# Attention and mixture of experts on one core: the products for the constant rows moved from one block in step 1 to eight groups in step 0, and the key rows cleared later

## What is computed

```python
attn = softmax(where(causal, -inf, q @ k.T * scale)); seq_out = attn @ v
x = layernorm(x + (seq_out + gated * mem_val) @ out_w.T + out_b)
h = gelu(x @ w1[e] + b1[e]); y = h @ w2[e] + b2[e]                # e = 0..3
c = einsum('eh,ehd->ed', gelu(b1), w2) + b2                      # one constant row for each expert
c_sum = c.sum(axis=0)
out = sum_k gates[k] * (y[topk[k]] - c[topk[k]] + c_sum)
x = layernorm(x + out)
```

## Time and profile before

| | |
|---|---|
| median of 3 runs | 1021.79 us (1018.55 to 1023.22) |
| the profiled execution | 1023.56 us, its span 1021.9 us |
| PE, PEld busy | 922.9 us (90%), 672.6 us (66%) |
| DVE, ACT, POOL busy | 736.5 us (72%), 595.0 us (58%), 425.8 us (42%) |
| mean granted TensorE clock | 0.961 of full |

### The profile page before, as it was taken

The page is one execution under the profiler, slowest core; times in us unless marked ns, Lnnn a source line. Parts: engine busy times, 40 slices in busy tenths (PEclk is TensorE's granted clock), DMA queues, the critical chain, the costliest instruction groups (busy, mean ns, idle before and its releaser), DMA issues. The chain is left out here.

```text
span 1021.9 us, 26568 instructions
## 1 busy us (share of the span) xinstructions
PE 922.9 (90%) x7976; PEld 672.6 (66%) x7977; DVE 736.5 (72%) x2689; ACT 595.0 (58%) x1357; POOL 425.8 (42%) x389
## 2 busy tenths in 40 slices
PE   4688999998899999999997989999999999999960
PEld 1244666656556666576564678888889978888850
DVE  4727789897787898989987677775655676555564
ACT  3246465564463555645555578676577756666663
POOL 6417144464183544644445534332222253233333
PEclk9789999999899999999999999999999999999985
DMA  4875203304114123041040543233223233233265
GB/s 147 259 203 141 64 23 95 96 22 141 51 53 137 43 89 102 1 137 53 22 146 2 184 163 82 51 48 49 43 43 71 47 85 53 42 52 52 39 191 180
DMA packets 60086, 89.48 MB, mean 88 GB/s; under 512 B 8636, under 2 KB 49488, under 8 KB 58928
## 3 DMA queue, kind: packets, MB, share of 16 engines
q1 hardware_dynamic: 44952, 61.80, 20.7%
q0 software_dynamic: 13728, 21.90, 11.3%
q10 hardware_dynamic: 1280, 4.19, 1.1%
HBM read 52.26 MB, written 35.47 MB: 86 GB/s over the span
## 5 line engine op out<-in xcount | busy, mean ns | idle before, releaser
L2007 DVE CUSTOM_DVE_ANT_0 junk<-sm,mask_ts 128x512 bf16<-128x512 f32 (+3 forms) x512 | 219.6, 486 | 59.4 <-PE sm L1405 58.0
L1145 ACT ACTIVATE arena_b<-st 128x512 f32<-128x512 f32 x320 | 180.2, 598 | 112.1 <-PE st L1367 111.0
L987 POOL DMA_INDIRECT sums<-arena_b x64 | 112.6, 1759 | 253.3 <-DVE arena_b L2241 243.3
L2203 DVE TENSOR_TENSOR arena_b<-arena_b 128x256 f16<-128x256 f32 (+1 forms) x280 | 116.1, 428 | 96.3 <-ACT arena_b L1221 93.9
L1365 PE MATMUL st<-arena_a 128*128 128x384 f16 (+3 forms) x512 | 127.0, 305 | 13.2 <-DMA arena_a<-max_row 7.5
L1405 PE MATMUL sm<-arena_a 128*128 128x512 f16 (+3 forms) x512 | 113.9, 310 | 12.8 <-DVE maxes L2007 6.5
L1556 PE MATMUL st<-arena_b,arena_a 128*128 128x256 f16 (+1 forms) x840 | 112.3, 271 | 6.4 <-DVE arena_b L1887 4.9
L1569 PE MATMUL pv<-arena_a,arena_b 128*128 x816 | 112.3, 274 | 0.0
L1556 PE MATMUL sm<-arena_b,arena_a 128*128 128x256 f16 (+1 forms) x840 | 110.7, 268 | 0.0
L1569 PE MATMUL sm<-arena_a,arena_b 128*128 x792 | 109.4, 274 | 0.0
L1217 ACT ACTIVATE arena_b<-sm,arena_b 128x256 f32<-128x256 f32 (+1 forms) x140 | 65.5, 468 | 65.8 <-PE sm L1556 50.6
(11 more groups left out here) (364 smaller groups left out, 1740.3 us busy)
## 6 DMA issues: line engine op xcount, KB each, us to landing
arena_b<-slots SPq DMA_DIRECT2D x32, 260.0 KB, 2.7
arena_a<-w SPq DMA_DIRECT2D x8, 1024.0 KB, 6.0
arena_b<-x_tr SPq DMA_DIRECT2D x8, 512.0 KB, 4.0
q_rows<-arena_b SPq DMA_DIRECT2D x32, 128.0 KB
k_rows<-arena_b SPq DMA_DIRECT2D x32, 128.0 KB
arena_a<-q_rows SPq DMA_DIRECT2D x32, 128.0 KB
arena_a<-k_rows SPq DMA_DIRECT2D x32, 128.0 KB
res<-x_tok POOLq DMA_DIRECT2D x8, 512.0 KB, 4.3
```

The costliest lines, as they stand in the source:

```text
L987: pool.indirect_dma_start(sums, bass.IndirectOffsetOnAxis(ap=token_now[:, 1 - par, m:m + 1], axis=0), y_out[1 - par][:, m, :], None, compu ...
L1145: act.activation(probs[:, q, :], st_ps[piece % 2][:, :], ACT.Exp, scale=SCORE_SCALE).then_inc(exp_done, 1)
L2007: last = dve.tensor_tensor_reduce(junk[:, n % 3, at:at + width], sm_ps[n % 3][:, at:at + width], mask_ts[:, T - width:T], 1.0, NEG, ALU.ad ...
L2203: dve.tensor_tensor(g_lo[par][:, hc, 0:rows], g_32[:, hc % 4, 0:rows], g_hi[par][:, hc, 0:rows], ALU.subtract).then_inc(hid_done, 1)
```

## The change

There are two parts.

First, the block of step 1 becomes eight groups in step 0. Stage `nothing` exists in step 0 and takes a number m from 0 to 7: group m is expert m // 2 and half m % 2 of its chunks, so four products, and it waits for its own transfer on `raw_in[m]` instead of `w2_in`, which is gone (the later use of `raw_in` in `weights` counts from 32). The groups stand in the list behind maxima 8, 10, 11, 13, 14 and 16, and the last two behind `maxima_rows`. ScalarE's copy stays where it was in step 1, as a stage of its own, `nothing_out`. Second, GpSimd waits for `dve_const` 4, VectorE's last instruction of the weights' split (L1646), before it clears `k_st[0]`; all that stands behind on GpSimd follows.

```diff
-        ("o_tokens", 2), ("scores", 3), ("nothing", 0), ("memory_scores", 0), ...
+        ("o_tokens", 2), ("scores", 3), ("nothing_out", 0), ("memory_scores", 0), ...
...
-        ("x1_rows", 1), ("values", 5), ("maxima", 8), ("maxima", 9), ("scores", 25), ("maxima", 10), ("scores", 26), ("x1_rows", 2),
+        ("x1_rows", 1), ("values", 5), ("maxima", 8), ("nothing", 0), ("maxima", 9), ("scores", 25), ("maxima", 10), ("nothing", 1), ("scores", 26), ("x1_rows", 2),
...
-        "first_rows": at == B, "load_w2": at == 0, "nothing": at == 1}
+        "first_rows": at == B, "load_w2": at == 0, "nothing": at == 0, "nothing_out": at == 1}
...
             split_x(0, 0)
+            pool.wait_ge(dve_const, 4)
             pool.memset(k_st[0][:, :, :, :].bitcast(F32), 0.0).then_inc(zeroed, 1)
...
-                    act.wait_ge(raw_in[n // 2], 16)
+                    act.wait_ge(raw_in[n // 2], 32)
...
-                            act.dma_start(w2_raw[2 * e + n], w_2[e, :, n, :].rearrange("p (a t) -> p a t", a=2)).then_inc(w2_in, 16)
+                            act.dma_start(w2_raw[2 * e + n], w_2[e, :, n, :].rearrange("p (a t) -> p a t", a=2)).then_inc(raw_in[2 * e + n], 16)
...
-                def expert_of_nothing(_):
-
-                    pe.wait_ge(w2_in, 32 * E)
-                    pe.wait_ge(gb_done, 1)
-                    pe.wait_ge(bias_done, 2)
-                    for hc in range(HC):
-                        for e in range(E):
-                            rows = w2_raw[2 * e + hc // 4][:, hc % 4 // 2, D * (hc % 2):D * (hc % 2) + D]
-                            last = pe.matmul(pv_ps[32 * e:32 * e + 32, 0:D], gb[:, HC * e + hc:HC * e + hc + 1].broadcast_to([P, 32]), rows,
-                                             start=hc == 0, stop=hc == HC - 1, skip_group_check=True)
-                    last.then_inc(c_ready, 1)
+                def expert_of_nothing(m):
+
+                    e, part = m // 2, m % 2
+                    if m == 0:
+                        pe.wait_ge(gb_done, 1)
+                        pe.wait_ge(bias_done, 2)
+                    pe.wait_ge(raw_in[m], 16)
+                    for hc in range(4 * part, 4 * part + 4):
+                        rows = w2_raw[m][:, hc % 4 // 2, D * (hc % 2):D * (hc % 2) + D]
+                        last = pe.matmul(pv_ps[32 * e:32 * e + 32, 0:D], gb[:, HC * e + hc:HC * e + hc + 1].broadcast_to([P, 32]), rows,
+                                         start=hc == 0, stop=hc == HC - 1, skip_group_check=True)
+                    if m == 2 * E - 1:
+                        last.then_inc(c_ready, 1)
```

More of the change, by code:

```diff
@@ L62, in stages_of_a_step @@
         ("late_maxima", 0), ("scores", 0), ("late_maxima", 1), ("o_tokens", 0), ("scores", 1), ("scores", 2), ("o_tokens", 1),
-        ("o_tokens", 2), ("scores", 3), ("nothing", 0), ("memory_scores", 0), ("o_tokens", 3), ("values_in", 0), ("scores", 4),
+        ("o_tokens", 2), ("scores", 3), ("nothing_out", 0), ("memory_scores", 0), ("o_tokens", 3), ("values_in", 0), ("scores", 4),
         ("scores", 5), ("late_maxima", 2), ("late_maxima", 3), ("values_in", 1), ("memory_gates", 0), ("scores", 6), ("scores", 7),
@@ L76, in stages_of_a_step @@
         ("scores", 23), ("first_weights", 1), ("maxima", 6), ("maxima", 7), ("normalise", 3), ("x1_rows", 0), ("scores", 24),
-        ("x1_rows", 1), ("values", 5), ("maxima", 8), ("maxima", 9), ("scores", 25), ("maxima", 10), ("scores", 26), ("x1_rows", 2),
-        ("x1_rows", 3), ("first_weights", 2), ("scores", 27), ("maxima", 11), ("maxima", 12), ("maxima", 13), ("scores", 28),
-        ("gates", 0), ("logits", 0), ("values", 6), ("scores", 29), ("scores", 30), ("maxima", 14), ("memory", 0), ("memory", 1),
-        ("first_weights", 3), ("maxima", 15), ("scores", 31), ("maxima", 16), ("tables", 0), ("scores", 32), ("values", 7),
+        ("x1_rows", 1), ("values", 5), ("maxima", 8), ("nothing", 0), ("maxima", 9), ("scores", 25), ("maxima", 10), ("nothing", 1), ("scores", 26), ("x1_rows", 2),
+        ("x1_rows", 3), ("first_weights", 2), ("scores", 27), ("maxima", 11), ("nothing", 2), ("maxima", 12), ("maxima", 13), ("nothing", 3), ("scores", 28),
+        ("gates", 0), ("logits", 0), ("values", 6), ("scores", 29), ("scores", 30), ("maxima", 14), ("nothing", 4), ("memory", 0), ("memory", 1),
+        ("first_weights", 3), ("maxima", 15), ("scores", 31), ("maxima", 16), ("nothing", 5), ("tables", 0), ("scores", 32), ("values", 7),
         ("maxima", 17), ("rank", 0), ("first_expert", 0), ("maxima", 18), ("scores", 33), ("memory", 2), ("maxima", 19), ("values", 8),
-        ("scores", 34), ("scores", 35), ("memory", 3), ("memory", 4), ("scores", 36), ("scores", 37), ("maxima_rows", 0), ("memory", 5),
+        ("scores", 34), ("scores", 35), ("memory", 3), ("memory", 4), ("scores", 36), ("scores", 37), ("maxima_rows", 0), ("nothing", 6), ("nothing", 7), ("memory", 5),
         ("first_rows", 0), ("scores", 38), ("values", 9), ("scores", 39), ("values", 10), ("values", 11),
@@ L457, in attention_and_ffn @@
         whi_done, wlo_done, table_done, table_chain, order_done = map(sem, ("whi_done", "wlo_done", "table_done", "table_chain", "order_done"))
-        w2_in = sem("w2_in")
         gb_done, c_ready, c_read, c_out, base_in, base_chain, base_done = map(sem, (
@@ L1186, in step @@
                             "last_memory_gates": lambda _: memory_gates(i - 2)}
-                run({"first_weights": weights, "load_w2": load_w2, "nothing": c_out_of_psum, "split": split_next, "values_in": values_in, "seed": seed, "normalise": normalise,
+                run({"first_weights": weights, "load_w2": load_w2, "nothing_out": c_out_of_psum, "split": split_next, "values_in": values_in, "seed": seed, "normalise": normalise,
                      "queries": lambda m: queries(i + 1, m), "tables": small_tables, "turn": turn, "z_rows": z_rows, "x1_rows": x1_rows, "lines_in": lines_out,
```

## The result

| | before | changed |
|---|---|---|
| median of the runs | 1022.26 us (4 runs, 1018.55 to 1023.22) | 1031.12 us (4 runs, 1030.11 to 1031.61) |
| profiled execution, its span | 1023.56, 1021.9 us | 1030.11, 1028.4 us |
| mean granted TensorE clock | 0.961 | 0.966 |

The ratio of the medians' comparison is 1.0088, 95% interval 1.0064 to 1.0111: slower by 6.5 to 11.3 us. The two profiled executions lie 6.55 us apart. The forecast was +6.7, 1028.5 us, slower.

The account below looks back on a forecast made before the run. Bound by VectorE's maxima pieces, TensorE's step 1 products, then SP's queue from the row of maxima to c_rows. Groups +6.9 including the prologue's -3.0, transposes -0.2: +6.7 us, 1028.5 us; range 1020.0 to 1033.5.

Parts of the forecast that it names:

- Step 1, the prologue: Prologue: later clearing of key rows frees VectorE from GpSimd's memsets; first maximum product 3.0 us earlier than 34.75.
- the two gains: Prologue: 3.1 us if the second low part's 3.26 us were partly queue time, only 0.75 if its own.
- Step 2, the groups: Step 0, groups 0 to 5: each 1.71 us at high clock; VectorE starves, last piece 57.8 instead of 50.86, +6.9.
- C: Step 0: one expert's products don't lift the low clock, groups cost 3.41 us each; total 1039; chance 0.08.
- D: Step 0: groups fit beside VectorE at 0.85 us each, so not slower; end 1020.6; chance 0.16.
- Step 3, groups 6 and 7: Step 0, TensorE's wait for the row of maxima: the two groups' 3.5 us hidden within 0.1.
- Step 4, step 1: Step 1: TensorE loses 4.87 us of products, but SP's queue moves +6.7; ScalarE's c_rows wait ends at 92.1.
- Rival B: SP's queue: crowded transfers shrink and the queue catches up, leaving only TensorE's +0.8; total 1022.6; chance 0.14.
- The sum: Whole kernel: prologue and step 0 groups +6.9, transposes -0.2, groups 6 and 7 nothing, saved 4.87 us lost waiting: +6.7.

Follow-up runs that it names:

- eight groups late: Changed kernel with all eight single groups moved behind step 0's row of maxima, instead of six ahead of it; ratio 1.001 (0.9987 to 1.0033).
- two packed groups: Changed kernel with its products as two groups, four experts side by side, behind step 0's row of maxima; late clearing kept; ratio 0.9987 (0.9963 to 1.001).

## Why the prediction was right

**Step 1, the prologue.** Predicted -3.0 us, first maximum product near 31.6, with the split on GpSimd late next. Measured 31.68 and -3.07, and the third burst did wait for the split, 5.49 us. The estimate of 1.86 us for the second low part, from the same operation on 1024 elements, was 0.08 too high. The rule of the Trainium skill's page SBUF — State Buffer, section "Who interferes with whom", told the right one of the two gains: the long cast and scaling were GpSimd's doing (2.53 and 3.33 us beside its memsets, 0.22 and 0.17 without). Whether the memset held the second low part only through the scaling ahead of it, which is what the page's rule leaves, or by itself, no run tells apart: both records of before end with the memset.

**Step 2, the groups.** 1.71 us a group plus 0.12 a change of form: the distance from a group to the next piece is 1.84, and a group starts 0.32 us behind the piece ahead of it (45.34 to 45.66) where a piece follows a piece in 0.22. The first group at the low clock was there, at 39.47 against 39.4, and the clock rose behind it. Last piece predicted at 57.8: its accumulator was read at 57.52. Until VectorE takes up piece 17, at 55.45, TensorE and no longer VectorE sets the pace. The row of maxima came 6.5 us later. Rivals C and D fall by these rows: the clock is high from the second group on, and no group costs 0.85.

**Step 3, groups 6 and 7.** Said to be hidden in the wait for the row of maxima, within 0.1 us. The row of 16 product records starts at 57.97, and the score piece that used to wait starts without one at 61.77, 3.29 us behind the store of the row, where it was 2.97 before (51.96 to 54.93). Hidden but for some 0.3 us.

**Step 4, step 1.** TensorE at the first values at 63.67, predicted 63.6. Of the queue, however, the term was mis-sized twice. I had it move by the same 6.7 us throughout. The first store of the query rows moved 6.0, the stores of c_rows 9.3, because the four stores of the key rows took 5.54 us to issue and not 3.41 and the loads behind them had to wait longer still; and c_rows then landed in 2.8 us instead of 7.5, so that the wait ended at 90.00 and not 92.1, 4.5 us later than before instead of 6.7. TensorE's wait behind it was 6.79 us, not 9. Why those stores landed so slowly in the profile of before isn't settled. On the second chip the stores of c_rows came 7.8 us later and landed in 2.6 us instead of 4.0, and the wait ended 6.4 us later. Rival B said that the queue might catch up: part of it did on the first chip, and far too little to take the loss away. What remained is the forecast's mechanism, groups that delay the row of maxima and with it the queue. The two kernels with the eight groups early and late bear it out; the load of the residuals moves between them too, and with it go 3.4 of the 13.7 us by which the stores of c_rows differ (section on the hardware).

**The sum.** +6.7 against +6.55 of the profiled pair and +8.9 (6.5 to 11.3) of the runs. The agreement with the pair is in part luck: +4.5 are direct in it, and 2 us arose among the experts, where I had nothing. Where the rest of the 8.9 arises isn't shown by any run here.

## What to carry to other kernels

Work moved to an engine that "waits anyway" is free only behind the last thing that others need from that stretch: put it behind the store that starts the next chain, not between the pieces ahead of it. Where one engine's early finish releases a transfer, look at which others it will fall among. And before an entry in a queue is pushed back, list who waits for it, not only who gains.

## What the hardware showed that I had not expected

**A load among stores, and stores that are late.** GpSimd's load of x_tok is released by ScalarE's copy of the products, so where the products stand decides when it goes out. In all fourteen traces, take the time from the first store of the query rows to the first load of the second sequence's rows. Where x_tok is issued 6.5 us or more behind that first store, it is 12.3 to 13.4 us (four traces, the profile before among them: 56.24 to 68.70). Where it comes 6.4 us behind or sooner, it is 15.7 to 16.2 (ten traces, the changed kernel among them: 62.21 to 78.11). The kernel with the eight groups late has it latest:

```profile
53.17 2.92 SPq L655 DMA_DIRECT2D q_rows<-arena_b  x4
...
65.51 0.32 SPq L681 DMA_DIRECT2D arena_a<-q_rows  x1
```

```profile
66.36 1.83 POOL L875 DMA_DIRECT2D res<-x_tok  x2 [28.82 <-ACT o_t L1182]
```

and the one with two packed groups has it early:

```profile
53.44 2.88 SPq L655 DMA_DIRECT2D q_rows<-arena_b  x4
...
69.19 0.32 SPq L681 DMA_DIRECT2D arena_a<-q_rows  x1
```

```profile
57.18 1.83 POOL L875 DMA_DIRECT2D res<-x_tok  x2 [19.90 <-ACT o_t L1182]
```

Where the load goes out early among the stores, the queue is thus some 3.4 us later (15.75 against 12.34 in the two kernels shown). That the load is the cause is not shown: the two go together in fourteen traces, and no run moved the load alone. If it is, it explains the early c_rows of the eight late groups, and why earlier products didn't give an earlier c_rows in full.

**Chips that are 4% slower with nearly the same clock and the same bytes.** The kernel before took 1060 to 1065 us on the three chips of the experiments, at a mean granted clock of 0.951 instead of 0.961 and with the same 89.48 MB moved. Its trace on the second of them has the mark 1.6 us earlier than the first profile, and then loses 38 us between 180 and 530 us, in steps of some 5 us, once or twice a sequence. They show on ScalarE and VectorE as waits for a releaser called "remote", which the first profile doesn't have in any row:

```profile
189.05 1.09 ACT L1145 ACTIVATE arena_b<-st 128x512 f32<-128x512 f32 x2 [4.61 <-remote]
```

What lies behind them isn't settled. They bound what the experiments can tell in the total: the runs of before spread by 11 to 15 us there, and the same kernel against itself came out at 1.0023.
